# Narrow attention over four stacked heads at a time, with transposed scores, in place of sixteen spread heads and a transposed softmax

## The reference

```python
# layer 2; layer 1 has q = x, k = v = context; layer 3 has biases bq, bk, bv and no mask
qh = (q @ wq).reshape(N, 256, 16, 8)
kh = (k @ wk).reshape(N, 64, 16, 8)
vh = (v @ wv).reshape(N, 64, 16, 8)
scores = jnp.einsum('nqha,nkha->nhqk', qh, kh)
scores = jnp.where(mask == 0, -1e10, scores)
attn = jax.nn.softmax(scores / math.sqrt(8), axis=-1)
out = jnp.einsum('nhqk,nkha->nqha', attn, vh).reshape(N, 256, 128) @ wo + bo
```

## Time and profile before

| | us |
|---|---|
| median of 3 runs (2042.43 to 2048.39) | 2042.72 |
| the profiled execution, its own time | 2044.18 |
| its span, first to last instruction | 2042.4 |
| narrow attention, layer 1 (first to last DVE instruction) | 403.15 to 581.69 |
| narrow attention, layer 2 | 885.97 to 1072.99 |
| narrow attention, layer 3 | 1630.24 to 1810.14 |

### The profile page before, as it was taken

How to read it: one execution, slowest core, us unless ns; L and a number is a source line. 1 busy time by engine, 2 the same in 40 slices (tenths; PEclk the granted TensorE clock), 3 DMA queues, 4 the chain that set the end, 5 groups by cost and what they waited for, 6 DMA issues and landing times. The chain is left out here.

```text
span 2042.4 us, 27863 instructions
## 1 busy us (share of the span) xinstructions
PE 1729.0 (85%) x9035; PEld 1284.5 (63%) x9035; DVE 1349.9 (66%) x3013; ACT 835.4 (41%) x1593; POOL 401.1 (20%) x329
## 2 busy tenths in 40 slices
PE   6999938999979999989995899999999889958004
PEld 5777727778956666658884666656666478843004
DVE  4777772177757667667764566666665577777885
ACT  3555523334435555533432322232232134326762
POOL 2110020055600000044561000000000055510320
PEclk9999967989979999989996999999999989979557
DMA  3000000010000000020000000000000000000000
GB/s 136 1 1 0 0 0 0 13 54 1 1 0 1 1 0 0 0 114 6 8 1 0 0 1 1 1 1 0 0 1 1 12 1 1 1 0 0 0 0 41
DMA packets 7749, 20.69 MB, mean 10 GB/s; under 512 B 2776, under 2 KB 4832, under 8 KB 6624
## 3 DMA queue, kind: packets, MB, share of 16 engines
q1 hardware_dynamic: 7648, 19.43, 2.5%
HBM read 17.33 MB, written 2.10 MB: 10 GB/s over the span
## 5 line engine op out<-in xcount | busy, mean ns | idle before, releaser
L797 PEld LDWEIGHTS psC_a<-vb_a,probs_a 128*128 128x128 f32 x1536 | 184.8, 197 | 0.0
L797 PE MATMUL psC_a<-vb_a,probs_a 128*128 128x18 f32 x1536 | 183.8, 263 | 0.0
L871 DVE TENSOR_REDUCE smax_a<-psS_a 128x16 f32<-128x1024 f32 x96 | 117.3, 1222 | 62.4 <-PE psS_a L777 62.4
L1642 ACT ACTIVATE xsh_f<-xs_f 128x512 fp32r<-128x512 f32 x120 | 75.8, 632 | 198.5 <-DVE xs_f L1895 198.3
L1895 DVE TENSOR_TENSOR xs_f<-xT_f,psR_f 128x512 f32<-128x512 f32 x128 | 86.8, 686 | 78.7 <-PE psR_f L1714 75.8
L2290 PE MATMUL ps_f<-wT_f,xq_f 128*128 128x128 f32 x192 | 24.2, 289 | 125.2 <-DVE xq_f L2311 125.2
L177 POOL TENSOR_TENSOR rstd_f<-vareps_f,mhalf 128x4 f32<-128x4 f32 x16 | 16.1, 1009 | 575.5 <-DVE vareps_f L163 575.5
L1758 PE MATMUL psX_f<-xs_f,wo_f2w 128*128 128x512 f32 x256 | 128.6, 594 | 0.0
L717 ACT ACTIVATE probs_a<-psS_a 128x1024 f32<-128x1024 f32 x96 | 98.3, 1024 | 72.6 <-PE psS_a L790 72.0
L1895 DVE TENSOR_TENSOR xs_f<-aoT_f,psR_f 128x512 f32<-128x512 f32 x128 | 85.8, 685 | 61.7 <-PE psR_f L1714 61.5
L1422 DVE SCALAR_TENSOR_TENSOR g_f<-psU_f,cols_f1w,t_f 128x512 f32<-128x512 f32 (+1 forms) x104 | 77.9, 749 | 72.6 <-ACT t_f L1235 70.4
(11 more groups left out here) (430 smaller groups left out, 4482.4 us busy)
## 6 DMA issues: line engine op xcount, KB each, us to landing
x_sb<-in_x SPq DMA_DIRECT2D x1, 2048.0 KB, 8.3
out<-x_sb SPq DMA_DIRECT2D x1, 2048.0 KB, 6.3
w_f1w<-in_F_w SPq DMA_DIRECT2D x2, 792.0 KB
ctxT<-in_ctxT SPq DMA_DIRECT2D x1, 1024.0 KB, 12.2
maskf_a<-in_mask SPq DMA_DIRECT2D x8, 128.0 KB, 2.3
self_f2w<-in_F_sel SPq DMA_DIRECT2D x1, 1024.0 KB
wq_f2w<-in_F_wq SPq DMA_DIRECT2D x1, 1024.0 KB
wk_f2w<-in_F_wk SPq DMA_DIRECT2D x1, 1024.0 KB
```

The source lines that it names most:

```text
L797: ins = nc.tensor.matmul(psC[g % 2][:, k * vw:(k + 1) * vw], probs[:, g % 2, k * P:(k + 1) * P], vb[:, g // TPI, g % TPI // 2, k, :], star ...
L871: nc.vector.tensor_reduce(smax[:, g % 2, :], by_head(psS[g % 2][:]), axis=AX.X, op=ALU.max)\
```

## The change

`narrow_attention` is rewritten. Its unit is a batch b: one sequence, two tiles (256 rows); there are 16 of them, all written out without a hardware loop.

- Four groups g of four heads, 32 rows each. SP copies, by SBUF-to-SBUF DMAs of 32 partitions x 512 columns, the rows of each group into `xs`: rows 0 to 31 and 32 to 63 the high part of the queries, rows 64 to 95 the low part. PE spreads the keys with a selection matrix (`front_k`), and ACT masks them into `ks` (rows: high, low, high; columns: 4 heads x 64 keys). One matmul over 96 rows then holds all three products for four heads.
- `scores(b, h)`: rows of x as output partitions, only to find the maxima (`largest`, DVE, 512 columns at a time). The maxima go into `mP`, are transposed (`max_T`, in a bank `psT` of their own) and written by ACT into rows 96 to 127 of `xs`, against rows of -1 in `ks`.
- `scores_T(b, g)`: the scores a second time, keys as output partitions, now over 128 rows with the maximum already taken off. `exp` reads them straight into `probs`. The shift on DVE and the eight transposes are gone.
- `heads_out(b)`: 32 columns of values (or of ones) as weights, 256 columns of probabilities moving; each group g writes its own 32 partitions of the bank `psV`. Values and sums have separate matmuls, 16 fp32 matmuls in all. `heads` come out transposed, so `heads_T` and `store_heads` go; the reciprocal is now of 128 x 256 elements.
- `front_kv` and POOL's spreading go; keys are projected once for the whole block, the bias of the values in layer 3 is folded into `bo` at the start. Layer 2 loads the mask in both orientations, and adds it with one bf16 matmul of 512 columns for each half of either kind of scores.
- Constants `sel`, `ones32`, `rowmask`, `dup` are loaded and converted beside layer 0's attention; `headmask` goes.

```diff
+GROUPS = 4
+GF = P // GROUPS
+GK = 4 * SC
+ST = BPI * P
+MAXROW = 3 * GF
...
+        ks = sb("ks", [P, 2, BPI, GROUPS, GK], F32R)
+        xs = sb("xs", [P, 2, GROUPS, T4], F32R)
+        qh, ql = sb("qh", [P, T4], F32R), sb("ql", [P, T4], F32R)
+        vs = sb("vs", [P, 2, BPI, PAIRS, GF])
         xn, xT = sb("xn", [P, TPI, P]), sb("xT", [P, T4])
-        qh, ql = sb("qh", [P, 2, T4], F32R), sb("ql", [P, 2, T4], F32R)
-        shifted, probs = sb("shifted", [P, 2, KEYS]), sb("probs", [P, 2, KEYS])
-        smax, rsum = sb("smax", [P, 2, H]), sb("rsum", [P, 2, H])
-        heads, headsT = sb("heads", [P, 2, P]), sb("headsT", [P, 2, P])
+        mP = sb("mP", [P, 2, 2, P])
+        probs = sb("probs", [P, 2, GROUPS, 2, ST])
+        heads = sb("heads", [P, 2, ST])
...
-                sp.dma_start(maskf[:], dram["mask"][:, bass.ds(j * TPI, TPI), :]).then_inc(s("wraw").sem, 16)
+            def stack(j):
+                if j >= 2:
+                    sp.wait_ge(s("scores_T").sem, s("scores_T").at(8 * (j - 1)))
+                sp.wait_ge(s("q_ready").sem, s("q_ready").at(j + 1))
+                for r in range(2):
+                    for g in range(GROUPS):
+                        sp.dma_start(xs[GF * r:GF * r + GF, j % 2, g, :].bitcast(F32), qh[GF * g:GF * g + GF, :].bitcast(F32))\
+                            .then_inc(s("stacked").sem, 16)
+                sp.wait_ge(s("q_split").sem, s("q_split").at(j + 1))
+                for g in range(GROUPS):
+                    sp.dma_start(xs[2 * GF:3 * GF, j % 2, g, :].bitcast(F32), ql[GF * g:GF * g + GF, :].bitcast(F32))\
+                        .then_inc(s("stacked_low").sem, 16)
             if masked:
-            if masked:
-                with sp.Fori(1, ITERS) as i:
-                    load_mask(i)
+            for j in range(ITERS):
+                stack(j)
+                if not j:
+                    ahead.start(pr, sp)
...
-                        store_heads(n - 1, g - 1)
+                nc.scalar.activation(qh[:], psF[:], ACT.Identity, bias=cols[:, 0:1]).then_inc(s("q_ready").sem, 1)
+
+            def front_v(j):
+                act.wait_ge(s("v_proj").sem, s("v_proj").at(j + 1))
+                if j >= 2:
+                    act.wait_ge(s("heads_out").sem, s("heads_out").at(2 * (j - 1)))
+                for b in range(BPI):
+                    v = psF[:, b * P:(b + 1) * P].rearrange("p (g e a d) -> p g e a d", e=2, a=2, d=dv)
+                    for e in range(2):
+                        for a in range(2):
...
+            def front_k(j, heads_of):
+                act.wait_ge(s("k_spread").sem, s("k_spread").at(j + 1))
+                if j >= 2:
+                    act.wait_ge(s("scores_T").sem, s("scores_T").at(8 * (j - 1)))
+                src = psP[0:MAXROW, :].rearrange("p (g b k) -> p b g k", g=GROUPS, b=BPI)
+                for h in heads_of:
+                    ins = nc.scalar.activation(ks[0:MAXROW, j % 2, :, :, h * SC:(h + 1) * SC], src, ACT.Copy,
+                                               scale=common["rowmask"][0:MAXROW, h:h + 1])
+                    ins.then_inc(s("k_ready").sem, 1)
+
+            def max_rows(b):
+                act.wait_ge(s("max_T").sem, s("max_T").at(b + 1))
+                j, p = b // 2, b % 2
+                nc.scalar.activation(xs[MAXROW:P, j % 2, :, p * ST:(p + 1) * ST],
+                                     psT[MAXROW:P, 0:ST].unsqueeze(1).broadcast_to([P - MAXROW, GROUPS, ST]), ACT.Copy)\
+                    .then_inc(s("max_ready").sem, 1)
+
+            def exp(b, g):
+                act.wait_ge(s("scores_T").sem, s("scores_T").at(4 * b + g + 1))
+                if b >= 2:
+                    act.wait_ge(s("heads_out").sem, s("heads_out").at(b - 1))
+                nc.scalar.activation(probs[:, b % 2, g, :, :], psX[g % 2][:].rearrange("p (e t) -> p e t", e=2), ACT.Exp,
+                                     scale=float(dv) ** -0.5).then_inc(s("probs").sem, 1)
...
+            for b in range(B):
+                j, p = b // 2, b % 2
+                exp(b, 0)
+                exp(b, 1)
+                if not p and j + 1 < ITERS:
+                    front_k(j + 1, range(2))
+                if p and j + 2 < ITERS:
+                    front_q(j + 2)
+                exp(b, 2)
+                if not p and j + 1 < ITERS:
+                    front_k(j + 1, range(2, 4))
+                exp(b, 3)
+                if b + 1 < B:
+                    max_rows(b + 1)
+                if not p and j + 2 < ITERS:
+                    front_x(j + 2)
+                if p and j + 1 < ITERS:
+                    front_v(j + 1)
             ahead.convert(pr, act)
...
+            def front_k(j):
+                for g in range(GROUPS):
+                    for m, part in enumerate((kh, kl)):
+                        ins = nc.tensor.matmul(psP[:, g * P:(g + 1) * P], sel[:, 4 * m + g, :], part[:, j * P:(j + 1) * P],
+                                               start=m == 0, stop=m == 1)
+                ins.then_inc(s("k_spread").sem, 1)
+
+            def scores(b, h):
+                j, p, c = b // 2, b % 2, h // 2
+                n = 4 * b + h
+                pe.wait_ge(s("maxed").sem, s("maxed").at(max(0, n - 1)))
+                if masked:
+                    nc.tensor.matmul(psY[h % 2][:], common["identb"][:],
+                                     maskb[:, j % 2, 0, (2 * p + c) * SC:(2 * p + c + 1) * SC].unsqueeze(1).broadcast_to([P, 8, SC]),
+                                     start=True, stop=False)
+                for e in range(2):
+                    g = 2 * (h % 2) + e
+                    t = p * ST + c * P
+                    ins = nc.tensor.matmul(psY[h % 2][:, e * GK:(e + 1) * GK], xs[0:MAXROW, j % 2, g, t:t + P],
+                                           ks[0:MAXROW, j % 2, p, g, :], start=not masked, stop=not masked or e == 1)
                 ins.then_inc(s("scores").sem, 1)
 
-            def front_done(j):
-                pe.wait_ge(s("q_split").sem, s("q_split").at(j + 1))
...
+            def max_T(b):
+                pe.wait_ge(s("maxed").sem, s("maxed").at(4 * b + 4))
+                if b:
+                    pe.wait_ge(s("max_ready").sem, s("max_ready").at(b))
+                for c in range(2):
+                    ins = nc.tensor.transpose(psT[:, c * P:(c + 1) * P], mP[:, b % 2, c, :], ident[:])
+                ins.then_inc(s("max_T").sem, 1)
+
+            def scores_T(b, g):
+                j, p = b // 2, b % 2
+                pe.wait_ge(s("max_ready").sem, s("max_ready").at(b + 1))
+                pe.wait_ge(s("probs").sem, s("probs").at(max(0, 4 * b + g - 1)))
+                if masked:
+                    nc.tensor.matmul(psX[g % 2][:], common["dup"][:, p, :],
+                                     maskb[:, j % 2, 1, :].unsqueeze(1).broadcast_to([P, 2, ST]), start=True, stop=False)
+                for e in range(2):
+                    ins = nc.tensor.matmul(psX[g % 2][:, e * ST:(e + 1) * ST], ks[:, j % 2, p, g, e * P:(e + 1) * P],
+                                           xs[:, j % 2, g, p * ST:(p + 1) * ST], start=not masked, stop=not masked or e == 1)
+                ins.then_inc(s("scores_T").sem, 1)
+
+            def heads_out(b):
+                j, p = b // 2, b % 2
+                pe.wait_ge(s("probs").sem, s("probs").at(4 * b + 4))
+                pe.wait_ge(s("v_ready").sem, s("v_ready").at(j + 1))
+                if b:
+                    pe.wait_ge(s("heads_norm").sem, s("heads_norm").at(b))
+                for part in range(2):
+                    for e in range(2):
+                        for g in range(GROUPS):
+                            left = ones[:, e, :] if part else vs[:, j % 2, p, 2 * g + e, :]
+                            ins = nc.tensor.matmul(psV[GF * g:GF * g + GF, part * ST:(part + 1) * ST], left,
+                                                   probs[:, b % 2, g, e, :], start=e == 0, stop=e == 1)
                 ins.then_inc(s("heads_out").sem, 1)
 
-            def heads_T(n, g):
-                pe.wait_ge(s("heads_norm").sem, s("heads_norm").at(n + 1))
-                nc.tensor.transpose(psC[g % 2][:, 256:256 + P], heads[:, g % 2, :], ident[:]).then_inc(s("heads_T").sem, 1)
...
+            def project(b):
+                pe.wait_ge(s("heads_norm").sem, s("heads_norm").at(b + 1))
+                for c in range(2):
+                    ins = nc.tensor.matmul(psP[:, c * P:(c + 1) * P], heads[:, b % 2, c * P:(c + 1) * P], wo, start=True, stop=True)
+                ins.then_inc(s("attn_proj").sem, 1)
...
+            for b in range(B):
+                j, p = b // 2, b % 2
+                more = b + 1 < B
+                scores_T(b, 0)
+                scores_T(b, 1)
+                if more:
+                    if p:
+                        stacks(j + 1)
+                    scores(b + 1, 0)
+                    scores(b + 1, 1)
+                if not p and j + 1 < ITERS:
```

(78 more changed lines are left out.)

397 lines of the change are left out of this document (154 added, 243 removed).

## The result

The changed kernel takes 2087.95 us (median of 4 runs, 2085.36 to 2089.36) where the kernel before takes 2043.9 beside it: a ratio of 1.021, 95% interval 1.019 to 1.023. It is slower by 44 us; I forecast 2035.5. The profiled execution took 2089.36 us, its span is 2087.2.

A forecast was written before the change was run, and what follows sets the result against it. PE was taken to bound the narrow attention stages, DVE next; layers 1 to 3 gave -11.6, +3.0 and -13.1 us, constants +1, clock +13.5: -7.2, so 2035.5 us against 2042.7, range 1990 to 2135 (own case 2012 to 2058).

The forecast's parts named there:

- the clock's term: Granted clock falling in some batches of narrow attention: between nothing and 3.5 us a batch, taken as 0.3, +13.5 us.
- the rival that describes what happened: The clock falls in nearly every batch because of its new wait: 2 us x 45 = +90, 2125 us; chance 0.13.
- The chain: From one fourth maximum to the next: `normalise`, PE's work, next scores, two maxima; 8.8 us a batch, 10.1 in layer 2.
- The reciprocal: In `normalise` on DVE, 256 elements at 6.4 ns per element: 1.8 us.
- The rival with a cheap reciprocal: Shorter chain: reciprocal at a product's cost, 0.42 us, takes 1.4 off; 0.9 x 45 less, 1995 us; chance 0.12.
- Heads-out: 32 fp32 matmul passes per batch on PE, four column groups side by side: 1.8 us, with 7.4 as upper end.
- both rivals with less overlap: `heads_out` groups overlap only by twos (3.6 us, 2116, chance 0.18) or not at all (7.4 us, 2285, chance 0.12).
- The stacking: The 12 stacking DMAs of two batches on SP: 12 x 0.47 + 2.3 = 7.9 us, hidden in the steady part.
- the cushion: Spare time of the stacking DMAs, wanted some 12 us after their start: 4 us, or 3 behind a mask's two loads.
- The first intervals and the tail: Layer 1: first two batches 7.1 and 7.6 us, tail 14.2; layer 2: 8 and 9 us, tail 16.
- the leads: Start of each stage until four maxima are done: 22 us in layer 1, 23 in layer 2.
- my own four signs for "wrong": `heads_out` at 3.6 or 7 us; steady clock under 0.95; PE awaiting DMA before an even batch's scores; ACT without gaps.

The follow-up runs named there:

- filled by half: The changed kernel with four added matmuls of 512 columns, results unread, ahead of `project`: 2035.85 us, ratio 0.9958 to the kernel before.
- project later: The changed kernel with `project(b-1)` and its add moved to the next iteration, behind its first two score groups: 2070.22 us, ratio 1.0134 to the kernel before.

## Why the prediction was wrong

The step that failed is the clock's term: "bursts between are dense, so I take 0.3". By stage, in us:

| | predicted without the clock | filled by half (steady clock 1.00) | changed kernel |
|---|---|---|---|
| layer 1 | 166.9 | 170.4 | 196.4 |
| layer 2 | 191.3 | 194.5 | 201.2 |
| layer 3 | 166.1 | 172.2 | 194.1 |
| sum | 524.3 | 537.1 | 591.7 |

The clock costs 591.7 - 537.1 = 54.6 us, 1.2 per batch in place of 0.3: 41 us of the miss. Everything else is off by 12.8 us. With the term right, the same sum gives 2035.5 + 41 = 2077, slower by 34 us. The sum stated its bounds for this term, 0 to 3.5; I chose near the lower one, and gave the rival that describes what happened 0.13. The 1.2 us are an average: 1.6 in layers 1 and 3, and 0.4 in layer 2, where the masks keep PE busier. The Trainium skill's TensorE: Matmul & The Clock Gate, Part 1, which I cited for a kernel that swings between both clocks, was the better guide than my choice: the trace shows that swing, 1.00 and 0.50 in turn.

So the sign of the forecast was wrong for one reason: I took a wait in every batch to be nearly free because the work between was dense, and the clock fell all the same.

The other steps, at the full clock:
- **The chain**: forecast 2.3 + 4.6 + 0.6 + 1.35 = 8.8. In the rows of the batch at 459 us: from the start of the reciprocal to `project` 461.63 - 459.28 = 2.35; from there to the scores 466.15 - 461.63 = 4.52; to the maximum 0.55; two maxima 467.90 - 466.70 = 1.20. Together 8.62. Right, each term to 0.15 us.
- **The reciprocal**: 1748 ns for 256 elements, forecast 1.8 from a slope of 6.4 ns per element. The rival with a cheap reciprocal falls. (Its price was mis-worked too: from 8.8 + 0.3 us a batch down to 7.6 with no loss to the clock is 1.5, not 0.9.) The count of 8 repeats in the Trainium skill's VectorE: DVE Perf Modes, in its account of the ALU slices, from which I estimated 2.1 us, is not what this row shows.
- **Heads-out**: 32 records in 466.15 - 464.29 = 1.86 us, forecast 1.8. All four groups run side by side, and both rivals with less overlap (3.6 and 7.4 us) fall. The nearest row, two row halves in other matmuls, pointed the right way. The order in the program matters: with the group as the outer loop the same records take 4.5 us. This agrees with the Trainium skill's TensorEngine Tiling (Array Packing), Key Properties, on tiles that run independently; the rate of up to four times, which I cited with it, stands in the same page's Overview. The drain at a change of tiling mode that Key Properties warns of is small here, on the way out: in layer 3 the scores start at 1753.49, 0.31 us behind the last four records of `heads_out` (1753.18), where four follow four in 0.22, so some 0.1 us.
- **The stacking**: the cushion was reckoned with 0.47 us per issue; it is 0.62 or more, so 12 issues and the landing (2.0 us) are 9.4 us, not 7.9. In the steady part of layers 1 and 3 it still fits. In layer 2 the second stacking cost 5.2 us where I had 4.
- **The first intervals and the tail** were too short, as the half filled kernel shows: 10.6 us to the second fourth maximum in layers 1 and 3 where I had 7.1 (DVE's list, above, which I left out), and 9.5 in layer 2 where I had 8; a tail of 17.1, 16.0 and 17.2 us where I had 14.2, 16 and 14.2. With the leads (3.8 us in all) and the third maximum of layer 2 (3.4) this is 21.6 us too little, of which the shorter steady batches give back 8.6.

Of my own four signs for "wrong" two came: a granted clock under 0.95 in the steady part, and, once, in layer 2, PE waiting for a DMA ahead of the first scores of an even batch (3.7 us). `heads_out` at 3.6 or 7 us and an ACT without gaps did not.

What stays open: why the clock falls about as much with a longest wait of 1.1 us (project later: 0.79 and 0.86 in layers 1 and 3) as with one of 1.8 (0.83 and 0.82), beside one of 0.5 in each. The runs show that more columns on PE in the same batch keep it up, and not which measure of its work decides.

## What to carry to other kernels

A change that takes work off PE until it waits in every batch must be priced at both clocks: here the loss to the clock, 1.2 us a batch, was larger than the 1.0 gained on the chain. Where such a wait can't be closed, matmuls whose result nobody reads, placed inside it and no longer than it, are worth a run: here four of 512 columns turned +2.1% into -0.4%, while the shorter chain without them stayed slower than the kernel before, at +1.3%. When matmuls are spread over column groups, let the groups alternate in the program: here it was 1.9 against 4.5 us.

## What the runs showed of the hardware

- The granted clock fell to half though in the steady part of layer 1 PE never waited more than 1.8 us at a time, and it did so periodically, every second batch there and every batch in layer 3. Four unread matmuls of 512 columns in each batch kept it at 1.00; the same four with 8 columns did not (0.83).
- Matmuls of 32 weight columns on four column groups started within 0.02 us of one another, and the next four 0.21 to 0.24 us on, also for fp32, whose matmuls have two records each. With a group's eight records in a row, the next group's first started beside the fifth, while the sixth to eighth, which stand ahead of it in the program, had not started.
- An SBUF-to-SBUF transfer of 64 KB held SP's queue for 0.59 us (median; 0.63 from one issue to the next), a load of weights from memory mostly for 0.43.
